# The last group of a 32-group transformer block: its two late transposes taken from TensorE to splits in rows and transposing transfers

## The reference, cut to what matters

```python
# attention over a segment, with a running memory over the segments
q, k, v = xs @ Wq, xs @ Wk, xs @ Wv
att_mem = sq @ mem / (sq @ z)                      # sq = elu(q) + 1
att_dot = softmax(q @ k.T * scale) @ v
att     = gate * att_mem + (1 - gate) * att_dot    # the attention rows
x = layernorm(x + att @ Wo)                        # the first norm
h = relu(x @ quantize(W1).T + b1)
x = layernorm(x + h @ quantize(W2).T + b2)
```

## Time and profile before

| | value |
|---|---|
| time, median of 3 runs | 1840.24 us |
| time of the profiled execution | 1839.69 us |
| span of the profiled execution, first to last instruction | 1837.9 us |
| mean granted TensorE clock | 0.990 |
| PE busy | 1783.5 us, 97% |
| DVE busy | 1461.5 us, 80% |
| ACT busy | 997.0 us, 54% |
| POOL busy | 781.8 us, 43% |

### The profile page before, as it was taken

The page is one execution under the profiler, slowest core; times in us unless marked ns, Lnnn a source line. Parts: engine busy times, 40 slices in busy tenths (PEclk is TensorE's granted clock), DMA queues, the critical chain, the costliest instruction groups (busy, mean ns, idle before and its releaser), DMA issues.

```text
span 1837.9 us, 42414 instructions
## 1 busy us (share of the span) xinstructions
PE 1783.5 (97%) x15935; PEld 1249.6 (68%) x15935; DVE 1461.5 (80%) x2807; ACT 997.0 (54%) x2422; POOL 781.8 (43%) x775
## 2 busy tenths in 40 slices
PE   4779999999999999999999999999999999999998
PEld 3556777766777766677766677766677776677765
DVE  7667788878888887888887888887878887888774
ACT  5765645555655555554655554655564555565542
POOL 0203444543444444354444354444344453444442
PEclk9889999999999999999999999999999999999999
DMA  8624435455445455435445534445543544443320
GB/s 281 150 38 78 74 73 90 59 88 87 73 76 93 61 84 91 83 67 90 71 72 93 86 66 85 77 66 94 87 71 78 86 63 89 89 74 73 60 47 24
DMA packets 555130, 150.87 MB, mean 82 GB/s; under 512 B 528544, under 2 KB 532528, under 8 KB 554416
## 3 DMA queue, kind: packets, MB, share of 16 engines
q1 hardware_dynamic: 554928, 148.16, 45.6%
HBM read 50.54 MB, written 16.80 MB: 37 GB/s over the span
## 4 chain that ended last, share of the span: by engine, by line
PE 95%; DVE 2%; ACT 2%; issue 1%; POOL 0%; DMA 0%; POOLq 0%; ACTq 0%; DVEq 0%
PE bank L464 12%; PE bank L465 12%; PE bank L448 12%; PE bank L449 12%; PE bank L294 6%; PE bank L295 6%; PE bank L296 6%; PE bank L378 3%; PE bank L426 3%; PE bank L428 3%; PE bank L427 3%; PE bank L308 3%; PE bank L310 3%; PE bank L309 3%; PE bank L413 2%; PE bank L327 1%
## 5 line engine op out<-in xcount | busy, mean ns | idle before, releaser
L448 PE MATMUL bank<-yt,w1t 128*128 128x256 f16 x2048 | 454.0, 273 | 0.6 <-ACT arena L1271 0.4
L449 PE MATMUL bank<-yt,w1t 128*128 128x256 f16 x2048 | 453.9, 273 | 0.0
L464 PE MATMUL bank<-w2t,arena 128*128 128x512 f16 x1024 | 388.7, 380 | 0.0
L465 PE MATMUL bank<-w2t,arena 128*128 128x512 f16 x1024 | 388.1, 379 | 0.0
L1271 ACT ACTIVATE arena<-bank,b_scaled,wscalars 128x256 f32<-128x256 f32 x512 | 261.2, 564 | 179.9 <-PE bank L449 108.6
L1215 ACT ACTIVATE bank<-bank,exp_bias,gscalars 128x128 f32<-128x128 f32 x512 | 220.5, 431 | 222.1 <-DVE exp_bias L752 222.1
L448 PEld LDWEIGHTS bank<-yt,w1t 128*128 128x128 f16 x2048 | 200.4, 98 | 24.2 <-ACT arena L1271 0.7
L449 PEld LDWEIGHTS bank<-yt,w1t 128*128 128x128 f16 x2048 | 200.4, 98 | 22.8
L875 DVE CAST arena<-arena 128x512 f16<-128x512 f32 x256 | 186.0, 727 | 7.5 <-ACT arena L1271 7.4
L1508 POOL TENSOR_TENSOR arena<-arena 128x512 f16<-128x512 f32 x128 | 155.2, 1213 | 68.6 <-DVE arena L875 68.6
L464 PEld LDWEIGHTS bank<-w2t,arena 128*128 128x128 f16 x1024 | 100.1, 98 | 118.6
(11 more groups left out here) (180 smaller groups left out, 4358.5 us busy)
## 6 DMA issues: line engine op xcount, KB each, us to landing
rows<-in_L_attn_x SPq DMA_DIRECT2D x32, 512.0 KB, 3.9
out_rows<-rows SPq DMA_DIRECT2D x64, 256.0 KB, 2.4
x_blocks<-in_L_attn_x SPq DMA_DIRECT2D x248, 64.0 KB, 3.0
sk<-sk_t SPq DMA_DIRECT2D x480, 32.0 KB, 2.0
arena<-in_L_ffn_W SPq DMA_DIRECT2D x6, 1024.0 KB, 5.6
w2t<-in_L_ffn_W SPq DMA_DIRECT2D x2, 1024.0 KB, 13.1
w1t<-in_L_ffn_W SPq DMA_DIRECT2D x2, 1024.0 KB, 14.2
amax_row<-amax_dram SPq DMA_DIRECT2D x31, 64.0 KB, 3.1
```

The source lines that it names most:

```text
L448: pe.matmul(ps[:, c], w1t[:, k, cols], yt[:, g % 2, :, k], start=k == 0, stop=False)
L449: ins = pe.matmul(ps[:, c], w1t[:, k, cols], yt[:, g % 2, :, KT + k], start=False, stop=k == KT - 1)
L464: pe.matmul(banks[own][:], h_hi[:, f, toks], w2t[:, f, :], start=f == 0, stop=False)
L465: ins = pe.matmul(banks[own][:], h_lo[:, f, toks], w2t[:, f, :], start=False, stop=f == FT - 1)
```

## The change

The last group is taken out of `EDGES`, and the four conditions that kept it out of the middle way are widened by one group. The last group's rows are then split in rows by ACT and POOL and turned by four transposing transfers of SP; its 16 PE transposes and its four subtractions on DVE are gone. Group 0 stays as it was. With `EDGES` the position of `at_hi(31, t)` on ACT moves from behind `h_relu(30, 5)` to ahead of it, `yt_hi(31, t)` takes its input from rows, and `add_bias(31, t)` waits for `yt_lo` in place of the PE transposes.

```diff
-        EDGES = (0, NG - 1)
+        EDGES = (0,)
...
             def at_lo(g, t):
-                if not 0 < g < NG - 1:
+                if not 0 < g < NG:
                     return
                 pool.wait_ge(sem["at_hi"], by_t(g, t))
...
             def yt_lo(g, t):
-                if not 0 < g < NG - 1:
+                if not 0 < g < NG:
                     return
                 pool.wait_ge(sem["yt_hi"], by_t(g, t))
...
             def turn_att(g, t):                    # SP
-                if not 0 < g < NG - 1:
+                if not 0 < g < NG:
                     return
                 sp.wait_ge(sem["at_lo"], by_middle(g, t))
...
             def turn_y(g, t):
-                if not 0 < g < NG - 1:
+                if not 0 < g < NG:
                     return
                 sp.wait_ge(sem["yt_lo"], by_middle(g, t))
```

## The result

The changed kernel takes 1842.56 us (median of 22 runs, 1841.05 to 1843.71), the kernel before 1839.82 us beside it (22 runs): 2.7 us more, a ratio of 1.0015 with a 95% interval of 1.0009 to 1.0021. That is inside the 0.2% that counted as no change, and the interval leaves out 1. The profiled execution took 1842.56 us with a span of 1840.8 us, 2.9 us over the span before.

A forecast was written before the change was run, and what follows sets the result against it. PE was taken as the bound, even in the drain. A later projection (2.15), less removed turns (0.87), plus clock loss (1.5) gave +2.8 us on 1840.24, so 1843.0 us, range 1840.6 to 1845.0.

The forecast's parts named there:

- The bound and the missing slack: PE in the drain: it bounds the kernel even there, and the output projection's operand `at` has no slack.
- The first tile: Group 31's attention rows, split on POOL then transferred: the output projection starts at 1786.4 instead of 1784.24, 2.15 us later.
- The second tile: Second tile of group 31's attention rows: its products follow the first tile's at once or within 0.2 us.
- The clock: PE's idle time of some 3.2 us before the output projection halves TensorE's clock: 1.5 us, bounds 0 and 3.3.
- The turns of the norm's rows: Two PE turns of the norm's rows among the `ffn_down` products come off the path: 0.87 us gained.
- What was costed at nothing: `h_rest(30, 7)`, the norm's transfers (2.8 us to spare) and group 29's stores on SP: all hidden, no cost.
- A: Rival: same wait before the output projection, but the clock never falls; 1841.5 us (1840.9 to 1842.5), chance 0.2.
- B: Rival: half speed outlasts the output projection, PE loses 3.3 us in `ffn_down(30, ...)`; 1844.8 us, chance 0.2.
- C: Rival: attention rows' transfer is in time, only the removed turns count; 1839.4 to 1840.7 us, chance 0.05.
- D: Rival: the change's conditions miss the group, so it does nothing; 1840.2 us, chance 0.02.

The follow-up runs named there:

- pool_early: The changed kernel, with POOL in pass 32 splitting group 31's attention rows ahead of `h_rest(30, 3)` and `add_bias(30, 0)`; 1838.97 us, ratio 0.9994 to the kernel before.
- fill14: The changed kernel plus 14 unread products on PE between `ffn_up(30, 7)` and the wait for the attention rows; 1841.33 us, ratio 1.0006 to the kernel before.
- y_only: The changed kernel with group 31's attention rows turned by PE again, only its norm's rows by transfers; 1839.23 us, ratio 0.9996 to the kernel before.
- att_only: The changed kernel with group 31's norm's rows turned by PE again, only its attention rows by transfers; 1843.72 us, ratio 1.0021 to the kernel before.

## Why the prediction was right

The forecast was 1843.0 us, the forecast range 1840.6 to 1845.0 and the sum +2.8 us; measured were 1842.56 and +2.7 (+2.9 in the span). Of the 0.44 us between forecast and time, 0.42 are the base: three runs gave 1840.24 for the kernel before, 22 gave 1839.82. The prediction also took 0.2% for about what can be told from no change; the 22 runs of each told 0.15%. Step by step:

- **The bound and the missing slack.** Right: all that the change did to the time is in PE's timeline, whose drain is 2.89 us longer where the span is 2.9 us longer.
- **The first tile.** POOL's split started at 1781.47 and took 1.60, the transfer 3.04 us from 1783.10, the release 0.14. The wait was read from the same rows: forecast start of the projection 1786.4, measured 1786.27; 2.15 late forecast, 2.07 measured. The key row was not the transfer's but POOL's: in `pool_early`, with POOL's place alone changed, the transfer starts 2.26 us sooner and the projection 2.09, which is the whole delay.
- **The second tile.** Right that it would follow at once; its split took 1.33. Here the slow products of the first tile helped; with the clock full, in `fill14`, it came 0.12 us late, within the 0.2 that the prediction allowed.
- **The clock.** Right that it would fall (the idle times of the prologue were the rows to go by), mis-sized by a little: 1.5 forecast, 1.70 measured. I had let part of the slow stretch pass while PE was still idle; it began only after the restart, so all of it, 1786.4 to 1789.8, was paid at half speed. The Trainium skill, page "TensorE: Matmul & The Clock Gate", section "HAM oscillation — how this bites in real kernels", tells of a wait for a transfer and products that start slow behind it. The trace agrees in this: a wait of 3.16 us, then 0.50.
- **The turns of the norm's rows.** -0.87 forecast, -0.88 measured, and `y_only` shows it alone: -0.86.
- **What was costed at nothing.** `h_rest(30, 7)` and the stores of group 29 held up nobody. The norm's transfers landed 3.2 us after their issue and not 4.3, so the spare time ahead of `ffn_up(31, 0)` was 3.6 us and not 2.8; the last is 1806.95 less 1800.1 + 3.2.
- **The rivals.** A (the clock stays) is `fill14` in its effect, 1.4 us over before; it did not happen in the profiled execution, though the lowest of the 22 times, 1841.05, would fit it, and no profile shows such an execution. B (a longer stretch at half speed) did not happen: the clock came back within the projection. C would have needed POOL to be free sooner, which is what `pool_early` gives it. D is out: PE has the 16 turns less.

## What to carry to other kernels

A scheme of the steady state carried into the drain loses what hid it there: here the next group's projections, behind which a split of 1.6 us and a transfer of 3.0 us had cost nothing. Before moving such a step, look what stands in front of its reader on every engine it passes, and give it an earlier place in the queues (POOL and ACT here) or needed work in front of the wait; either turned +2.7 us into about -2 (-2.1 and -1.8). Price a wait of PE of some 3 us at more than itself: with the slow stretch behind it, it cost 1.7 us more (waits of 3.16 and 3.17 us; behind one of 1.08 us the clock stayed).

## What the runs showed that I had not expected

- Fourteen useless products on PE made the changed kernel 1.3 us faster (1.4 over the kernel before instead of 2.7), since they kept the clock.
- The stretch at half speed begins after PE has started again: full while idle from 1783.1 to 1786.3, then 0.50 to 1789.8. In `att_only` it begins 0.9 us behind the restart, near 1787.4, and costs the same. It isn't always so: in the prologue of the kernel before, the clock fell near 37.9 while PE stood idle from 35.5 to 39.0.
- A transposing transfer of 3.0 us took 4.48 us in one execution of four of the same kernel; what was issued around it, the first tile's transfer ahead and the stores of group 29 behind, is the same in all four. The two stores took 2.12 us to issue there and 1.28 in the other three, so the hold-up was not this transfer's alone.
